# Expert-list scatters of a routed layer: other split points, slot words in two buffers, running places placed elsewhere in the order

## The reference, cut to what matters

```python
h = concatenate([tok(A, B, x, log_dt, 512), softmax(catid)[x_txt]], axis=1)   # 16 x 192 x 512
h = h + attn(layernorm(h), W_in, conv_w, conv_b, dt_bias, A_log, D, norm_w, W_out)
h = h + ffn(layernorm(h), gate_weight, gate_up_proj, down_proj, similarity)
```

## Time and profile before

| | us |
|---|---|
| median of three runs | 1774.24 |
| profiled execution, its own time | 1780.81 |
| span of the profile, first to last instruction | 1779.1 |
| mean granted TensorE clock (1 is 2.4 GHz) | 0.917 |
| TensorE busy / VectorE / POOL / ScalarE | 1574.6 / 971.2 / 781.5 / 730.3 |
| list scatters L1016, 192 of them | 219.9 busy, 59.0 idle before them |
| state products, gates and other work of the layer stage | about 416 to 1137 |
| first instruction of the expert stage on POOL | 1146.00 |

### The profile page before, as it was taken

How to read it: one execution, slowest core, us unless ns; L and a number is a source line. 1 busy time by engine, 2 the same in 40 slices (tenths; PEclk the granted TensorE clock), 3 DMA queues, 4 the chain that set the end, 5 groups by cost and what they waited for, 6 DMA issues and landing times. The chain is left out here.

```text
span 1779.1 us, 31373 instructions
## 1 busy us (share of the span) xinstructions
PE 1574.6 (89%) x9263; PEld 1146.1 (64%) x9264; DVE 971.2 (55%) x2325; ACT 730.3 (41%) x1592; POOL 781.5 (44%) x638
## 2 busy tenths in 40 slices
PE   7999999997599999999999670099999999999996
PEld 7999999975477576675766340066655666666564
DVE  5555554523768998889789545034333343433443
ACT  2525253522776765857658100033333333333332
POOL 4230300011042357677675567545544555555554
PEclk9999999988799998998899575599999999999999
DMA  7210000003355352443423110167767777777665
GB/s 267 77 60 1 13 1 13 1 18 134 114 152 143 93 153 77 134 130 93 151 64 90 27 37 2 60 181 190 159 154 188 162 181 167 169 183 182 162 114 92
DMA packets 97703, 195.20 MB, mean 110 GB/s; under 512 B 38391, under 2 KB 46879, under 8 KB 92880
## 3 DMA queue, kind: packets, MB, share of 16 engines
q0 software_dynamic: 36992, 88.26, 23.1%
q1 hardware_dynamic: 60624, 105.78, 19.5%
HBM read 144.15 MB, written 49.84 MB: 109 GB/s over the span
## 5 line engine op out<-in xcount | busy, mean ns | idle before, releaser
L1888 PE MATMUL moe_ps_gu<-moe_wgu,moe_xt 128*128 x960 | 331.9, 489 | 0.0
L1746 POOL DMA_INDIRECT out_h<-moe_yy,moe_idx_s x121 | 190.9, 1578 | 256.2 <-DVE moe_idx_s L1808 117.4
L1016 POOL DMA_INDIRECT scratch_slots<-lay_toki,lay_slot x192 | 219.9, 1145 | 59.0 <-issue 58.1
L1888 PEld LDWEIGHTS moe_ps_gu<-moe_wgu,moe_xt 128*128 128x128 f32 x960 | 173.7, 191 | 96.6 <-issue 1.2
L1785 ACT ACTIVATE moe_sl<-moe_ps_gu 128x192 f32<-128x192 f32 x120 | 39.7, 331 | 365.7 <-PE moe_ps_gu L1888 336.2
L1411 DVE SCALAR_TENSOR_TENSOR lay_xa<-lay_ring,head_cw,lay_xa 128x378 f32<-128x378 f32 (+5 forms) x240 | 141.9, 609 | 54.4 <-ACT lay_xa L1068 46.0
L1197 PE MATMUL lay_ring<-lay_xnt,win_sb 128*128 128x128 f32 (+2 forms) x1152 | 167.6, 292 | 4.3 <-DVE lay_xa L1411 2.0
L1281 PE MATMUL lay_ring<-head_wout,lay_yb 128*128 128x512 f32 x384 | 170.1, 597 | 0.0
L1197 PEld LDWEIGHTS lay_ring<-lay_xnt,win_sb 128*128 128x128 f32 (+2 forms) x1152 | 150.6, 200 | 10.5 <-issue 3.8
L1740 POOL DMA_INDIRECT moe_xg<-scratch_xg,moe_idx_g x123 | 131.4, 1069 | 47.5 <-issue 28.7
L247 POOL TENSOR_TENSOR tok_vv<-tok_w 128x512 f32<-128x512 f32 x16 | 16.6, 1040 | 259.7 <-ACT tok_w L449 225.5
(11 more groups left out here) (290 smaller groups left out, 2961.5 us busy)
## 6 DMA issues: line engine op xcount, KB each, us to landing
lay_m<-scratch_cum SPq DMA_DIRECT2D x16, 1536.0 KB
moe_wgu<-in_wgu SPq DMA_DIRECT2D x32, 768.0 KB
moe_wd<-in_wd SPq DMA_DIRECT2D x32, 384.0 KB
out_h<-lay_hres SPq DMA_DIRECT2D x48, 128.0 KB
scratch_xg<-lay_x SPq DMA_DIRECT2D x48, 128.0 KB
win_sb<-in_win SPq DMA_DIRECT2D x1, 4384.0 KB, 16.3
tok_u_raw<-in_tok_u SPq DMA_DIRECT2D x16, 256.0 KB, 4.5
tok_v_raw<-in_tok_v SPq DMA_DIRECT2D x16, 256.0 KB, 5.1
```

The source lines that it names most:

```text
L1016: pool.indirect_dma_start(out=a["slots"], out_offset=bass.IndirectOffsetOnAxis(ap=slot[:, j, k:k + 1], axis=0), in_=toki[:, j:j + 1], in_o ...
L1746: pool.indirect_dma_start(out=a["out"], out_offset=bass.IndirectOffsetOnAxis(ap=idx_s[n][:, 0:1], axis=0), in_=yy[n][:], in_offset=None, b ...
L1888: last = mm(ps_gu[b][:], xt[b][:, t], wgu[:, bass.ds(r * KD + t, 1)].rearrange("p o n -> p (o n)"), start=t == 0, stop=t == KD - 1)
```

## The change

Four edits, all in the layer stage:

- The groups of scatters of a late list become 5, 7, 4, 8 (they were 3, 3, 4, 14), and 5, 4, 11, 4 in pass 7, the one without a next pair.
- `slot`, `toki` and the semaphore `scat` exist twice and are used in turn; the waits are for the list two before.
- `places(w)` of pairs 0 to 5 stands behind the fourth z projection instead of in front of the first, in TensorE's order and in the ring's.
- For pair 6 TensorE's `places` stands between the second and the third output product of pass 7, VectorE's `router_columns` in front of the residuals, its counts and places behind the second residual. Pair 7's order on TensorE stays; on VectorE its three parts keep their order with nothing between them in pass 8.

```diff
@@ -694,6 +694,8 @@
 
 XZ_ORDER = [("z", k) for k in range(MI)] + [("x", k) for k in range(MI)]
 
+PL_BEHIND = 4
+
 
 FF = 192
 
@@ -717,17 +719,22 @@
         n = i + 1
         if 0 <= i < PAIRS:
             order += [("y", i, k) for k in range(N_Y)]
+        if n < PAIRS:
+            order += [(c, n, k) for c, k in XZ_ORDER[:PL_BEHIND]]
         if 0 <= i - 2 < PAIRS - 2:
             order.append(("pl", i - 2, 0))
         if n < PAIRS:
-            order += [(c, n, k) for c, k in XZ_ORDER]
-        if 0 <= i < PAIRS:
-            order += [("o", i, j) for j in range(N_BLK)]
+            order += [(c, n, k) for c, k in XZ_ORDER[PL_BEHIND:]]
+        for j in range(N_BLK):
+            if 0 <= i < PAIRS:
+                order.append(("o", i, j))
+            if j == 1 and i == PAIRS - 1:
+                order.append(("pl", i - 1, 0))
         if n < PAIRS:
             order += [("xt", n, k) for k in range(N_XT)]
         if n + 1 < PAIRS:
             order += [("bc", n + 1, 0), ("bc", n + 1, 1)]
-        if i - 1 >= PAIRS - 2:
+        if i == PAIRS:
             order.append(("pl", i - 1, 0))
     return order
 
@@ -791,8 +798,8 @@
         posi = s.sb("posi", [P, 3, TOPK], I32)
         hif = s.sb("hif", [P, 3, TOPK])
         slotf = s.sb("slotf", [P, 3, TOPK])
-        slot = s.sb("slot", [P, 3, TOPK], I32)
-        toki = s.sb("toki", [P, 3], I32)
+        slot = [s.sb(f"slot{n}", [P, 3, TOPK], I32) for n in range(2)]
+        toki = [s.sb(f"toki{n}", [P, 3], I32) for n in range(2)]
 
         gf = s.sb("gf", [P, 2])
         cnti = s.sb("cnti", [P, E], I32)
@@ -875,7 +882,8 @@
         h_out = s.sem("h_out")
         x2_out = s.sem("x2_out")
         w_out = s.sem("w_out")
-        scat = s.sem("scat")
+
+        scat = [s.sem(f"scat{n}") for n in range(2)]
         counted = s.sem("counted")
         ready = s.sem("ready")
         table_out = s.sem("table_out")
@@ -1004,24 +1012,27 @@
 
                 def list_places(k):
                     pool.wait_ge(slot_done, k + 1)
-                    if k:
-                        pool.wait_ge(scat, k * (3 * TOPK * 16))
+                    if k >= 2:
+                        pool.wait_ge(scat[k % 2], k // 2 * (3 * TOPK * 16))
                     nc.gpsimd.tensor_tensor(slotf[:], posk[:], on[:], ALU.add).then_inc(listed, 1)
                     pool.wait_ge(listed, k + 1)
-                    own.step(nc.gpsimd.tensor_copy(slot[:], slotf[:]))
-
-                def fill_lists(first, last):
+                    own.step(nc.gpsimd.tensor_copy(slot[k % 2][:], slotf[:]))
+
+                def fill_lists(i, first, last):
                     for q in range(first, last):
                         j, k = q // TOPK, q % TOPK
                         pool.indirect_dma_start(
-                            out=a["slots"], out_offset=bass.IndirectOffsetOnAxis(ap=slot[:, j, k:k + 1], axis=0),
-                            in_=toki[:, j:j + 1], in_offset=None,
-                            bounds_check=P * SLOT_COLS - 1, oob_is_err=False).then_inc(scat, 16)
+                            out=a["slots"], out_offset=bass.IndirectOffsetOnAxis(ap=slot[i % 2][:, j, k:k + 1], axis=0),
+                            in_=toki[i % 2][:, j:j + 1], in_offset=None,
+                            bounds_check=P * SLOT_COLS - 1, oob_is_err=False).then_inc(scat[i % 2], 16)
 
                 project_text(0)
                 text_rows(0)
                 for i in range(-1, PAIRS + 1):
                     n, r, w = i + 1, i - 1, i - 2
+
+
+                    cuts = (0, 5, 12, 16, 3 * TOPK) if pairs(n) else (0, 5, 9, 20, 3 * TOPK)
                     if pairs(i):
                         gate_y(i, 0)
                         gate_y(i, 1)
@@ -1032,27 +1043,28 @@
                     if pairs(n) and n:
                         text_rows(n)
                     if listed_late(w):
-                        fill_lists(0, 3)
+                        fill_lists(w, cuts[0], cuts[1])
                     if pairs(i):
                         square_sums(i)
                     if pairs(n + 1):
                         project_text(n + 1)
                     if listed_late(w):
-                        fill_lists(3, 6)
+                        fill_lists(w, cuts[1], cuts[2])
                     if pairs(i):
                         pool.wait_ge(ssv_done, i + 1)
                         nc.gpsimd.tensor_tensor(rr[:], ssv[:], mhalf[:], ALU.pow).then_inc(rr_done, 1)
                     if listed_late(w):
-                        fill_lists(6, 10)
+                        fill_lists(w, cuts[2], cuts[3])
                     if pairs(i):
                         pool.wait_ge(ve2_done, i + 1)
                         nc.gpsimd.tensor_tensor(rstd[:], ve[:], mhalf[:], ALU.pow).then_inc(rstd2_done, 1)
                     if listed_late(w):
-                        fill_lists(10, 24)
+                        fill_lists(w, cuts[3], cuts[4])
                     if listed_early(r):
                         list_places(r)
-                        fill_lists(0, 24)
-                pool.wait_ge(scat, PAIRS * 3 * TOPK * 16)
+                        fill_lists(r, 0, 3 * TOPK)
+                for n in range(2):
+                    pool.wait_ge(scat[n], PAIRS // 2 * 3 * TOPK * 16)
 
             @block.scalar
             def _(act):
@@ -1330,11 +1342,12 @@
                                 routed_rows(r, m2)
                             if m2:
                                 router_logits(r, m2 - 1)
-                    if listed_late(w):
-                        places(w)
+                    for k in range(MI):
+                        if k == PL_BEHIND and listed_late(w):
+                            places(w)
+                        if pairs(n):
+                            project(n, "z", k, COL_Z + k * P, P)
                     if pairs(n):
-                        for k in range(MI):
-                            project(n, "z", k, COL_Z + k * P, P)
                         pe.wait_ge(td_in_done, n + 1)
                         if pairs(r):
                             pe.wait_ge(x2t_done, r * 3 + 3)
@@ -1355,6 +1368,8 @@
                         output(i, 0)
                         square_columns(i)
                         output(i, 1)
+                    if listed_early(r) and pairs(i):
+                        places(r)
                     if pairs(n + 1):
                         token_rows(n + 1)
                     if pairs(i):
@@ -1364,7 +1379,7 @@
                             x_transposes(n, k)
                     if pairs(n + 1):
                         project_bc(n + 1)
-                    if listed_early(r):
+                    if listed_early(r) and not pairs(i):
                         places(r)
                 pe.wait_ge(ssv_done, PAIRS)
                 pe.wait_ge(macc_done, PAIRS)
@@ -1545,9 +1560,9 @@
                     own.step(v.tensor_scalar(posk[:], posk[:], float(SLOT_COLS), None, ALU.mult))
                     own.step(v.scalar_tensor_tensor(posk[:], hif[:], -float(P * SLOT_COLS - 1), posk[:], ALU.mult, ALU.add))
                     own.step(v.scalar_tensor_tensor(posk[:], topf[:], float(EXP_TILES), posk[:], ALU.mult, ALU.add))
-                    if k:
-                        dve.wait_ge(scat, k * (3 * TOPK * 16))
-                    own.mark(v.tensor_copy(toki[:], tokf[:]))
+                    if k >= 2:
+                        dve.wait_ge(scat[k % 2], k // 2 * (3 * TOPK * 16))
+                    own.mark(v.tensor_copy(toki[k % 2][:], tokf[:]))
                     v.tensor_scalar(on[:], on[:], -1.0e6, 1.0e6, ALU.mult, ALU.add).then_inc(slot_done, 1)
                     own.step(v.tensor_scalar(tokf[:], tokf[:], float(2 * SEQ), None, ALU.add))
 
@@ -1632,21 +1647,21 @@
                         router_weights(r)
                     if pairs(i):
                         square_columns(i)
+                    if listed_early(r):
+                        router_columns(r)
                     if pairs(n):
                         state_matrix(n, 0)
                     for j in range(N_BLK):
                         if pairs(i):
                             residual(i, j)
+                        if listed_early(r) and j == 1:
+                            router_counts(r)
+                            router_places(r)
                     for k in range(N_XT):
                         if pairs(n):
                             x_dt(n, k)
-                    if listed_early(r):
-                        router_columns(r)
                     if pairs(i):
                         routed_shift(i)
-                    if listed_early(r):
-                        router_counts(r)
-                        router_places(r)
                     if pairs(n + 1):
                         conv(n + 1, 0)
                         conv(n + 1, 1)
```

## The result

| first measurement | before | after |
|---|---|---|
| median, us | 1774.72 (1768.41 to 1785.33, 4 runs) | 1795.49 (1788.02 to 1799.15, 4 runs) |
| profiled execution: time / span | 1780.81 / 1779.1 | 1799.15 / 1797.4 |
| ratio after / before | | 1.0102, 95% interval 1.0064 to 1.0140 |

The account below looks back on a forecast made before the run. POOL's list scatters were taken to bound the layer stage's last 75 us, with TensorE busiest overall (89%). Terms -13.3 - 6.5 + 2.9 + 3.0 = -13.9 us against the median 1774.24 gave 1760.3; forecast 1760, range 1747 to 1770.

Parts of the forecast that it names:

- tail term: Last passes of the layer stage: four POOL waits around lists 5 to 7 vanish, 13.3 us gained; bounds 9 and 13.5.
- list 7 from VectorE: Rival, chance 0.05: in the tail, list 7's words come 4 us late; tail gains 9 instead of 13.3, time 1765.
- Late releases: Pass ends: a last train of 8 scatters instead of 14 removes half of VectorE's 13.1 us idle, 6.5 gained.
- full release: Rival, chance 0.2: all 13.1 us at the pass ends come and TensorE keeps 2.4 GHz; 1748 to 1754.
- Powers: Passes 2 to 5: more scatters ahead delay the first powers, the residual starts late; cost 3.0 us, bounds 0 and 5.
- Places: Passes 2 to 6: VectorE's counts wait for places behind the fourth z projection; net cost 2.9 us, bounds 0 and 26.
- Slower: Rival, chance 0.06: thirty scatters moved beside VectorE's busiest stretch in five passes hold VectorE, up to 29.4 us; 1790.
- no release: Rival, chance 0.2: the lateness at the pass ends is TensorE's own, nothing gained there; sum -7.4 us, 1767.
- the whole sum: Layer stage, all terms together: -13.3 - 6.5 + 2.9 + 3.0 = -13.9 us.
- theory T: Follow-up experiments' theory: during an unbroken scatter train, TensorE's release of a waiting engine comes late, at latest when the train ends.

Follow-up runs that it names:

- D: Chip of three sets of follow-up runs; the kernel before took 1787.6 to 1791.5 us there, the unaltered changed kernel 1793.11, 1798.79 and 1798.70.
- B: Chip of one set of follow-up runs; the unaltered changed kernel took 1750.69 us there, ratio 0.9916 to the kernel before.
- only_lists: Changed kernel with the places made ahead of the z projections again, on chip B: 1751.04 us, ratio 0.9909 to the kernel before.
- C: Chip of one set of follow-up runs; the unaltered changed kernel had ratio 0.9917 to the kernel before there.
- hold: Changed kernel with list 6's 24 scatters held until VectorE has read pair 7's router logits, on chip A: 1755.88 us, ratio 0.9945.
- A: Chip of one set of follow-up runs, all of altered versions of the changed kernel; the one with list 6 held had ratio 0.9945 there.
- hold_c: Changed kernel with list 6's scatters held until VectorE has read pair 7's logits, on chip D: 1777.80 us, ratio 0.9927.
- hold4: Changed kernel with 4 of list 6's scatters sent at once, 20 held until pair 7's logits are read, on chip D: 1781.43 us, ratio 0.9954.
- cuts_only_b: Kernel before with the new scatter cuts alone, one buffer and places where they were, on chip D: 1776.51 us, ratio 0.9921.
- again_d: Changed kernel unaltered, on chip D beside the kernel with list 6 held: 1798.79 us, ratio 1.0050 to the kernel before.
- again_e: Changed kernel unaltered, on chip D beside the kernel with 20 of list 6's scatters held: 1798.70 us, ratio 1.0067 to the kernel before.
- again_c: Changed kernel unaltered, on chip D beside the changed kernel with the old scatter cuts: 1793.11 us, ratio 1.0012 to the kernel before.
- cuts_only: Kernel before with the new scatter cuts alone, one buffer and places where they were, on chip C: ratio 0.9911.
- the additions: Changed kernel with list 6 after list 7 and 28 POOL additions of 128x384 in list 6's old place, on chip A: 1789.25 us, one run.

## Why the prediction was wrong

**The step that failed** is one sentence of the tail term: that list 7's words are there at 1090.5 because VectorE goes on from the last logits, "one microsecond of slack". I priced that chain at up to 4 us longer (list 7 from VectorE, 0.05). The chain itself was right, 24.0 against 24.3; its start was 22.7 us late (logits ended at 1067.97, read at 1090.68; forecast 1065.8 for both). I had the late releases before me, tied them to scatter trains, and counted them only as a gain where trains were taken away. The tail now has 39 scatters from 1036.98 to 1088.66, none starting more than 1.4 us after the end of the one before, and puts the release on which everything waits inside it. In the kernel before, VectorE stood at the landing wait anyway until 1070.50, so that any lateness of the logits of 1062.64 was hidden, and this was the last release before the new train:

```profile
1070.50 0.17 DVE L1550 CAST lay_toki<-head_tokf 128x3 int32<-128x3 f32 x1 [13.22 <-DMA scratch_slots<-lay_toki,lay_slot]
```

It looks as if the wait that the change removed had been doing work. The cuts alone, which keep it, are on time on D; that no other part of the change matters is argued, not shown.

**Tail, -13.3.** Measured +13.5 in the first measurement; on B 137.4 against 146.2, and from list 5's first words (996.51 and 998.73) to the expert stage -15.3. Where releases are on time the term is right within 2 us, list 7 starts with no idle time, and the slack is 3 us.

**Late releases, -6.5 of 13.1.** The four in the y stretch are gone, as the rows of pass 7 show (before 998.51 with 4.96 of idle time):

```profile
992.37 0.74 DVE L1438 SCALAR_TENSOR_TENSOR lay_yb<-lay_xa,head_dcol,lay_ring 128x192 f32<-128x192 f32 x2 [2.01 <-PE lay_ring L1228]
994.61 0.74 DVE L1438 SCALAR_TENSOR_TENSOR lay_yb<-lay_xa,head_dcol,lay_ring 128x192 f32<-128x192 f32 x2 [1.50 <-PE lay_ring L1228]
```

But passes 1 to 6 gained nothing (442.82 against 442.42): ScalarE, which reads the x projections, was late instead. The train over them now has seven transfers, two gathers of text rows and five scatters (three before), and its last late release comes 0.5 to 1.2 us after the last scatter in passes 2, 4, 5 and 6 (here 5 and 6; the scatters before them end at 871.21 and 947.36):

```profile
872.40 1.23 ACT L1080 ACTIVATE lay_xa<-lay_ring,head_cb,head_cw 128x384 f32<-128x384 f32 x2 [2.93 <-remote]
...
948.57 0.67 ACT L1080 ACTIVATE lay_xa<-lay_ring,head_cb,head_cw 128x384 f32<-128x384 f32 x1 [1.53 <-PE lay_ring L1214]
```

ScalarE's waits before this instruction sum to 29.2 us in passes 1 to 6 of the changed kernel, 15.8 in the kernel before, and 8.8 in either kernel on B. That was the "against" of my own rival, full release ("the new trains of 7 may make the same further up"). On B, with none to release, the gate of pass 7 came 7.9 us sooner, but the list words, 0.9 ahead in pass 2, were only 2.2 ahead in pass 7: 1.4 us over five passes. So this term came to nothing where nothing is late.

**Powers, +3.0.** Right in size: in the changed kernel the first powers take 3.1 to 3.2 in passes 2 to 5 and the residual waits 0.8 for them in each, 3.1 in all (pass 3, POOL and VectorE):

```profile
743.07 3.17 POOL L1055 TENSOR_TENSOR lay_rr<-lay_ssv,head_mhalf 128x3 f32<-128x3 f32 x1
```
```profile
746.27 0.75 DVE L1476 SCALAR_TENSOR_TENSOR lay_hres<-lay_ring,lay_rr,lay_hres 128x512 f32<-128x512 f32 x1 [0.78 <-POOL lay_rr L1055]
```

On B they take 1.4 and nothing waits.

**Places, +2.9.** Too high: VectorE waited 0.24 and 0.58, in passes 4 and 6, and nothing elsewhere; with the move undone, the time does not change measurably (only_lists).

```profile
778.82 0.26 DVE L1545 COPY lay_pos<-lay_ring 128x96 f32<-128x96 f32 x1 [0.24 <-PE lay_ring L1285]
```

**Slower, 0.06.** The outcome was on that side, by another mechanism. VectorE's product beside the scatters is unchanged: its eight instances have a mean of 3351 ns in all four traces (both kernels, first measurement and B). Nor did the order matter: in pass 3 of the changed kernel a scatter began 0.94 us ahead of the product, and it was the scatter that was drawn out, from 0.98 to 1.88 us:

```profile
741.19 1.88 POOL L1024 DMA_INDIRECT scratch_slots<-lay_toki,lay_slot  x1 [0.30 <-issue]
```
```profile
742.13 3.35 DVE L1454 SCALAR_TENSOR_TENSOR lay_m<-lay_m,lay_gm 128x3072 f32<-128x3072 f32 x1
```

The kernel before had such a case too (a scatter of 4.66 us at 832.96, the product's halves at 833.35), so my "the trace shows only the other order" was wrong. The rule of the Trainium skill, page "SBUF — State Buffer", section "Who interferes with whom", that the order of issue decides who blocks, has no case against VectorE here.

The sum without the late releases, -13.3 + 2.9 + 3.0 = -7.4, was the rival "no release"; the medians on B and C differ by 16.5 and 16.0. That the -13.9 of the whole sum is near these is luck: late releases, powers and places came to nothing there, and the tail, with 15.3 from list 5's words on, brought nearly all.

## What to carry to other kernels

A wait that an engine meets while another is late anyway can be what keeps a train of scatters off a critical release: before removing it, follow the one wait on which the stage ends and ask what GpSimd is issuing when it is released. Where a trace already shows releases that outlast their producer's record, price them on every wait that the change moves into such a stretch, not only where it takes them away. And a ratio of 1% from one chip can have the other sign on the next; here the cuts alone give 0.991 on C and 0.992 on D, the whole change 0.992 on B and C, 1.001 to 1.007 on D and 1.010 in the first measurement.

## What the runs showed of the hardware

**It is not only TensorE.** After list 7's words VectorE makes the tile table, 34 small instructions that nearly all wait for VectorE's own signal. From the start of the first to that of the last it took 7.3 to 7.9 us in every trace but two, hold on A among them, in the midst of a train. In hold_c and hold4 on D it lay 18 scatters or more behind the start of a train and took 32.4 and 31.0, with many of the instructions 0.7 or 1.4 us apart instead of 0.2. Its first and last instruction and one between, of hold_c:

```profile
1090.09 0.19 DVE L1573 TENSOR_SCALAR lay_prod<-lay_ps_g 128x32 f32<-128x32 f32 x1
...
1095.76 0.22 DVE L1583 TENSOR_REDUCE lay_mx<-lay_prod 128x2 f32<-128x64 f32 x1 [1.87 <-remote]
...
1122.47 0.14 DVE L1612 TENSOR_SCALAR iters<-iters 1x1 int32<-1x1 int32 x1 [1.26 <-DVE iters L1611]
```

There the expert stage opened 4 and 6 us later (13.33 and 15.71 idle before the memset against 9.5).

**It depends on how far the train has gone.** On D two kernels show releases on time well into a train: behind a pause of 3.3 us (cuts_only_b, from 1068.68) up to the places, read at 1093.09 during the 19th scatter, and behind one of 5.6 us (hold_c, from 1066.52) up to list 7's words at 1089.70, some 18 scatters on. The next late one in cuts_only_b stands between two trains: VectorE started on the counts only at 1103.04, though TensorE's record of them ends at 1094.32 and VectorE's own instruction before had ended by 1101.11. The trace does not tell which of these two releases it was. TensorE, then VectorE:

```profile
1094.13 0.19 PE L1372 MATMUL lay_ps_g<-macc,head_ones_b 128*128 128x32 bf16 x1 [1.07 <-issue]
```
```profile
1103.04 0.19 DVE L1557 TENSOR_SCALAR lay_prod<-lay_ps_g 128x32 f32<-128x32 f32 x1 [1.94 <-remote]
```

In the unaltered kernel, whose 39 scatters have no such pause in them, the logits' release was 16 to 19 us late on D and 22.7 in the first measurement. The end of the train is not what lets it through, as theory T had it: the read came 2.0 us behind the last scatter in the first measurement, 4.3 and 4.2 behind it in again_d and again_e, and 4.4 before its end in again_c. All this would fit something that fills faster than it drains. That is argued, not shown; nothing in the traces names it: the scatters of list 6 take 0.98 us and 1.28 a step on every chip, and list 5 or 6 landed as fast on D as elsewhere (2.1 us of POOL's time before the next words in cuts_only_b, 1.6 to 2.6 in cuts_only on C).

**Open:** why D shows it and A, B, C don't; whether other long work of POOL would hold a release on D, since the additions ran on A only; what the landing wait alone is worth there; whether the first measurement was on D, which its late releases and its times (1774.7 before; D 1787.6 to 1791.5, the others 1765.8 to 1767.2) leave undecided.
